# A 4-layer transformer block stack on one core: natural query and key rows, heads split at the eviction, a reworked block inversion and new order tables

## The chip, the cores and the metric

The kernel is one program on one core of a Trainium2 chip. The metric is the device time of one execution in microseconds (us). Everything is float32, apart from two small masks in bfloat16.

## The reference, cut to what matters

64 sequences of 128 tokens and 128 channels pass through four layers; each layer is an attention, a cross-attention on a context of 77 tokens and a feed-forward part, each with a residual and a layer norm:

```python
x = _layernorm(x + _L0_attn_ref(x, ...))        # "rec": a recurrence over the tokens, called memory below
x = _layernorm(x + _L0_xattn_ref(ctx, x, ...))  # "x0": 16 heads of 8 channels, softmax
x = _layernorm(x + _L0_ffn_ref(x, ...))         # "f0": routed experts
x = _layernorm(x + _L1_attn_ref(x, ...))        # "a1": latent attention
x = _layernorm(x + _L1_xattn_ref(x, ctx, mask)) # "x1": 16 heads of 8, masked
x = _layernorm(x + _L1_ffn_ref(x, ...))         # "f1"
x = _layernorm(x + _L2_attn_ref(x, ...))        # "a2": 16 heads of 8
x = _layernorm(x + _L2_xattn_ref(x, ctx, ...))  # "x2": 16 heads of 8, masked
x = _layernorm(x + _L2_ffn_ref(x, ...))         # "f2"
x = _layernorm(x + _L3_attn_ref(x, ...))        # "a3": 16 heads of 8, rotary
x = _layernorm(x + _L3_xattn_ref(x, ctx, ...))  # "x3": relu attention
x = _layernorm(x + _L3_ffn_ref(x, ...))         # "f3": conv, 16 heads of 8, gated experts
```

The heads of 8 channels are what the first part of the change touches: six stages (x0, x1, a2, x2, a3, f3) compute `softmax(q k^T) v` for 16 heads of 8 channels. The recurrence of `rec` needs, for each sequence, the inverse of a unit triangular system of 128 tokens, which the kernel solves in four blocks of 32 tokens; this is the second part.

## The kernel before, in words

There are two phases. The **opening** (`opening`, class `Memory`, from the start to 463.6 us) works on all 64 sequences at once and computes the memory `z` of `rec`, which goes to DRAM; beside it run steps that prepare weights (`Setup`, `setup_*`). The **main part** (`decoder_phase`) handles 16 batches of 4 sequences. Three groups (threads 0, 1, 2) hold one batch each and walk through the twelve stages; their instructions are interleaved on every engine by a table written out by hand into the file (`ORDER`, one character for each step of a thread; `MEMORY_ORDER` for the opening; `in_order` runs them). The order on an engine is fixed, so an instruction that waits holds up all three threads. `BATCH` lists the steps of a batch on each engine and gives the semaphore values, `GIVEN` says which pair of PSUM banks goes to which stage.

**The opening.** From 0 to 84 us the keys of all sequences are made (`keys_*_of`, three threads). Then come four blocks of 32 tokens:
- `g` is copied from PSUM (L1078), stored to DRAM and loaded back as `E`, one sequence in each of 64 partitions (L1128, L1132).
- The elimination (`memory_vector`, L1083 to L1099) takes 31 steps j. With n = 31 - j each is a chain of four VectorE instructions: a reciprocal (L1087), a column of n values (L1090), an outer product n x n into `outer` (L1093) and a subtraction n x n (L1097). GpSimd (`memory_gpsimd`, L1045 and L1049) carries the inverse along: an outer product and a subtraction of n x (j + 1) values in each step, which wait for the column of L1090.
- VectorE turns the inverse into `xx` twice, negated and scaled (L1104, L1107). It is stored (L1135) and loaded back by eight DMAs into the diagonal blocks of a 128 x 128 operand `xs` (L1143).
- TensorE multiplies with it (`next_pairs`, L955; 128 rows, 32 matmuls for four chunks of 4 x 4 sequences each), ScalarE and VectorE copy each chunk (L1014, L1071), `next_diagonal` (L970) completes the next `g`.
- Beside the elimination of the next block runs what is left of this one (`rest_tensor`, `rest_scalar`: L863 to L884, L899 to L910) and `early_diagonal` (L922, L926).

After the fourth block 16 products (L997) give the last part of `z`; it stays in `uT`, which is stored whole, 4 MB (L1152), and the main part begins.

**The attention stages.** Each of 16 heads has 8 rows, and a matmul of the scores works on a 32-row strip of queries and keys (L1525, L1551). For that the queries and keys are projected with padded weights: two matmuls, one for each half of the heads (t = 0, 1), with zero rows between (`queries_tensor` L1495, `keys_tensor` L1426); in a3 four each, since the rotary partner is a projection too (L2387). ScalarE evicts each half of the queries with its bias (L1504). Of the keys VectorE evicts the first half (L1443) and ScalarE the second (L1440), two copies each, one for every head of a pair, with the other head's rows zeroed. The maxima of the scores (L1617) go to free rows of `tops`, are transposed by one TensorE instruction (L1537) and added to both halves of the queries (L1620), after which the scores are computed a second time, keys first, with the maximum subtracted (L1551), and exponentiated (L1604).

```python
for t in range(2):                                     # queries_tensor, L1492 to L1496
    e.matmul(b.bank[st][t][:, :], g.w.part(st + "_q", t), src, ...)
```

## Time and profile before

| | us |
|---|---|
| median of 3 runs | 5462.85 (5457.16 to 5479.28) |
| profiled execution | 5466.28, its span 5464.1 |
| opening, to the first DMA issue of the main part | 463.6 |
| main part | 5000.5 |
| granted TensorE clock, mean | 0.94 |

| engine | busy us | share |
|---|---|---|
| TensorE matmul | 4782.4 | 88% |
| VectorE | 3585.9 | 66% |
| ScalarE | 2303.5 | 42% |
| GpSimd | 705.7 | 13% |

How to read it: a float32 matmul leaves two records in the trace, a transpose leaves one. Records of TensorE overlap, so its busy time is less than count times mean. In views by line, each group gives busy time and mean duration of one record, and after the bar the idle time before it and what ended that. "L1495" is line 1495 of the kernel. The span starts at the first instruction.

### The profile page before, as it was taken

What the parts mean: (1) busy time and instruction counts of PE and PEld (TensorE: products, weight loads), DVE (VectorE), ACT (ScalarE), POOL (GpSimd) and SP (SyncE); (2) the same over time, 40 slices, a digit from 0 to 9 for tenths busy, and PEclk for the clock granted to TensorE, in tenths of its full rate; (3) what the DMA queues carried; (4) which work ended last, traced back from release to release, by engine and by line L of the source; (5) the groups of instructions that cost most, each with busy time, mean ns of one, the idle gap of its engine ahead of it and who ended that gap; (6) DMA issues with size and microseconds to landing.
All of it is one profiled execution on the core that took longest, in us unless ns stands there. A gap on an engine that the chain in (4) does not pass through costs nothing.

```text
span 5464.1 us, 130532 instructions
## 1 busy us (share of the span) xinstructions
PE 4782.4 (88%) x55217; PEld 3486.1 (64%) x55217; DVE 3585.9 (66%) x9609; ACT 2303.5 (42%) x4635; POOL 705.7 (13%) x738
## 2 busy tenths in 40 slices
PE   5574889899998989999999999999999989988787
PEld 4453666566766666776766676666676766666555
DVE  7664477666667676667776576767767677756643
ACT  3111344444434454453554444454445355343432
POOL 5452000101000010110010010011110010100010
PEclk7676899999999999999999999999999999999998
DMA  1103101011110101111100111010021110110001
GB/s 61 23 17 105 58 7 32 2 32 31 51 53 20 32 3 40 60 44 41 33 2 19 41 54 48 26 33 15 28 63 41 32 33 10 32 43 22 2 24 37
DMA packets 144930, 184.57 MB, mean 34 GB/s; under 512 B 46074, under 2 KB 73826, under 8 KB 143714
## 3 DMA queue, kind: packets, MB, share of 16 engines
q1 hardware_dynamic: 144354, 176.23, 10.7%
q8 instruction: 442, 7.24, 0.5%
q14 instruction: 134, 1.10, 0.1%
HBM read 164.32 MB, written 11.57 MB: 32 GB/s over the span
## 4 chain that ended last, share of the span: by engine, by line
PE 63%; DVE 12%; issue 7%; ACT 6%; POOL 1%; DMA 1%; SPq 1%; POOLq 0%; DVEq 0%; ACTq 0%
PE g_bank L2649 8%; PE g_bank L2664 8%; PE g_bank L1551 6%; PE g_bank L1574 5%; PE g_bank L1525 4%; ACT g_keys_exps L1604 4%; DVE g_tops L1617 3%; PE g_bank L1495 2%; PE g_bank L1901 2%; PE g_bank L1911 2%; PE g_bank L2387 2%; PE g_bank L1426 2%; PE g_bank L1381 1%; PE g_bank L1994 1%; PE g_bank L2249 1%
## 5 line engine op out<-in xcount | busy, mean ns | idle before, releaser
L1604 ACT ACTIVATE g_keys_exps<-g_bank 128x512 f32<-128x512 f32 (+1 forms) x1536 | 796.0, 596 | 601.6 <-PE g_bank L1551 600.8
L1617 DVE TENSOR_REDUCE g_tops<-g_bank 128x4 f32<-128x512 f32 (+1 forms) x1536 | 808.5, 575 | 318.9 <-PE g_bank L1525 316.6
L1360 POOL TENSOR_TENSOR g_rstd<-g_rstd,minus_half 128x4 f32<-128x4 f32 x224 | 227.2, 1015 | 4144.2 <-DVE g_rstd L1342 4103.0
L2664 PEld LDWEIGHTS g_bank<-region,g_keys_exps 128*128 128x128 f32 x4096 | 517.3, 192 | 151.4 <-issue 140.6
L2649 PE MATMUL g_bank<-g_xT,region 128*128 128x512 f32 x1024 | 550.7, 619 | 8.6 <-DVE g_keys_exps L2689 4.2
L2664 PE MATMUL g_bank<-region,g_keys_exps 128*128 128x128 f32 x4096 | 546.4, 278 | 3.7 <-DVE g_base L2696 3.7
L1551 PE MATMUL g_bank<-g_qa,g_keys_exps 32*77 32x128 f32 (+1 forms) x12288 | 455.8, 285 | 53.7 <-DVE g_o L1638 34.2
L1551 PEld LDWEIGHTS g_bank<-g_qa,g_keys_exps 32*77 32x77 f32 (+1 forms) x12288 | 379.8, 169 | 158.8 <-DVE g_o L1638 57.0
L1574 PE MATMUL g_bank<-g_keys_exps,g_v 77*32 77x128 f32 (+1 forms) x12288 | 430.7, 283 | 39.7 <-DVE g_tops L1617 28.9
L1525 PE MATMUL g_bank<-g_keys_exps,g_qa 32*128 32x154 f32 (+1 forms) x6144 | 389.3, 365 | 77.3 <-ACT g_keys_exps L1604 67.4
L1574 PEld LDWEIGHTS g_bank<-g_keys_exps,g_v 77*32 77x32 f32 (+1 forms) x12288 | 324.8, 112 | 145.3 <-DVE g_tops L1617 84.7
L1525 PEld LDWEIGHTS g_bank<-g_keys_exps,g_qa 32*128 32x128 f32 x6144 | 262.1, 189 | 190.5 <-ACT g_keys_exps L1604 112.1
L2677 ACT ACTIVATE g_keys_exps<-g_bank,region 128x512 f32<-128x512 f32 x256 | 176.0, 687 | 447.5 <-PE g_bank L2649 447.2
L2689 DVE TENSOR_SCALAR g_keys_exps<-g_bank,region 128x512 f32<-128x512 f32 x256 | 191.5, 748 | 241.5 <-PE g_bank L2649 240.3
L1598 ACT ACTIVATE g_oT_sc<-g_bank 128x256 f32<-128x256 f32 x384 | 146.8, 383 | 373.0 <-PE g_bank L1574 372.6
L1620 DVE TENSOR_TENSOR g_qa<-g_qa,g_bank 128x256 f32<-128x256 f32 x384 | 159.9, 416 | 180.2 <-PE g_bank L1537 177.7
L1369 ACT ACTIVATE g_x<-g_x,g_shift,g_rstd 128x128 f32<-128x128 f32 x384 | 170.5, 488 | 160.5 <-DVE g_shift L1346 159.4
L2649 PEld LDWEIGHTS g_bank<-g_xT,region 128*128 128x128 f32 x1024 | 158.5, 192 | 59.2 <-issue 45.7
L1635 DVE RECIPROCAL g_total<-g_bank 128x16 f32<-128x16 f32 x384 | 95.9, 250 | 131.7 <-PE g_bank L1585 131.0
L1585 PE MATMUL g_bank<-consts_sb,g_oT_sc 128*128 128x128 f32 x768 | 159.5, 292 | 23.1 <-ACT g_keys_exps L1604 11.7
L1335 DVE BATCH_NORM_STATS2 g_stats<-g_x 128x6 f32<-128x128 f32 x768 | 176.5, 279 | 3.6
L2696 DVE SCALAR_TENSOR_TENSOR g_base<-g_bank,g_gates,g_base 128x128 f32<-128x128 f32 x512 | 149.3, 342 | 43.3 <-PE g_bank L2664 38.4
(375 smaller groups left out, 8771.3 us busy)
## 6 DMA issues: line engine op xcount, KB each, us to landing
region<-L_w_in SPq DMA_DIRECT2D x512, 256.0 KB, 3.0
region<-xT_in SPq DMA_DIRECT2D x16, 256.0 KB, 2.7
z_scratch<-m_uT SPq DMA_DIRECT2D x1, 4096.0 KB, 11.0
g_oT_sc<-z_scratch SPq DMA_DIRECT2D x16, 256.0 KB, 3.0
g_xT<-xT_in SPq DMA_DIRECT2D x16, 256.0 KB, 3.9
g_o<-x_in SPq DMA_DIRECT2D x16, 256.0 KB, 4.0
out<-g_x SPq DMA_DIRECT2D x16, 256.0 KB, 2.4
region<-weights_in SPq DMA_DIRECT2D x1, 3020.5 KB, 10.2
```

The lines of the kernel that those rows point to most:

```text
L1335: e.bn_stats(g.stats[:, n, :], src[:, n, :]).then_inc(*b.vector(f"{st} stats {n}"))
L1360: e.tensor_tensor(g.rstd[:, :], g.rstd[:, :], g.s["minus_half"], ALU.pow).then_inc(*b.gpsimd(st + " rstd"))
L1369: e.activation(out[:, n, :], src[:, n, :], ACT.Identity, bias=g.shift[:, n:n + 1], scale=g.rstd[:, n:n + 1]).then_inc(*b.scalar(f"{st} nor ...
L1525: ins = e.matmul(bank[r][:, 2 * nk * t:2 * nk * (t + 1)].rearrange("p (i k) -> p i k", i=2), g.qa[rows, t, n, :], g.km[rows, n, t, :, 0:nk ...
L1551: ins = e.matmul(bank[r][0:nk, u * T:(u + 1) * T], g.km[rows, n, t, i, 0:nk], g.qa[rows, t, n, :], start=not masked, stop=not masked or u ...
L1574: ins = e.matmul(b.bank[st][0][32 * u:32 * u + 32, k * T:(k + 1) * T], g.v[0:nk, n, 8 * i + 4 * k + u, :], g.p[0:nk, 2 * i + k, u, :], sta ...
L1604: e.activation(g.p[0:nk, r, :, :], bank[r][0:nk, :].rearrange("p (u q) -> p u q", u=4), ACT.Exp, scale=scale).then_inc(*b.scalar(f"{st} p ...
L1617: e.tensor_reduce(g.tops[:, first:first + 4].rearrange("p (t i) -> p t i", t=2), src, AX, ALU.max).then_inc(*b.vector(f"{st} top {n} {r}"))
L2649: e.matmul(bank[0][:, :], weights.part(f"w1 {x}", c), g.xT, start=True, stop=True).then_inc(*b.tensor(f"f3 hidden {k}"))
L2664: ins = e.matmul(bank[1][:, n * D:(n + 1) * D], g.gated_hid[:, x % 2, c, n * T:(n + 1) * T], weights.part(f"w2 {x}", c), start=c == n == 0 ...
L2677: e.activation(g.gated_hid[:, k // HC % 2, k % HC, :], b.bank["ex"][0][:, :], ACT.Relu, bias=g.w["f3_b1"][:, k:k + 1]).then_inc(*b.scalar( ...
L2689: e.tensor_scalar(g.gated_hid[:, x % 2, k % HC, :], b.bank["ex"][0][:, :], g.w["f3_b1"][:, k:k + 1], 0.0, ALU.add, ALU.max).then_inc(*b.ve ...
```

## The change

Three things are changed together.

1. *Natural rows.* Head h keeps its own 8 rows of the 128 (32-row strips hold four heads, t is their half of the strip). Queries and keys are projected once with the plain weights; the split is made where PSUM is evicted, with a per-partition scale that is 1 or 0 (`half` for queries, `own_head` for keys). x1 keeps two key projections, because its mask needs two rows (`own_or_mask`). In x0 and x2 all four key copies are ScalarE's; in a2 and f3 ScalarE's two wait for VectorE's two, since both read one bank; a3 has four projections rather than eight, four products with the rotary table rather than eight, two additions on GpSimd rather than four, and ScalarE makes the two halves of the queries from SBUF. The maxima lie in different free rows for the two halves, so they are transposed by two instructions rather than one.
2. *The opening.* The column of a step is no VectorE instruction: ScalarE makes it for GpSimd (`columns_scalar`), and VectorE's outer product takes the reciprocal as its scalar (`scalar_tensor_tensor`); for n up to 22 it is written to PSUM. The inverse is kept transposed in two buffers `XT`, with the reciprocals in a 33rd column, and is stored as it is, 264 KB; two DMAs (1,024 pieces of 132 bytes each) bring it back to a compact `xs`. Products use 32-row, 32-column tiles. The scaling by the reciprocals is done where V and s are made. z is transposed by TensorE, kept for one block (`z`) and stored block by block, so that 1 MB is left at the end; a batch loads it by four DMAs. The solve of the next four sequences is issued ahead of the rows of the current ones (`solve_tensor`). The stores and loads of a block come ahead of the ten small setup DMAs on SyncE's queue. ScalarE's table places one column step after every one to three steps of its other work.
3. *Tables.* `MEMORY_ORDER`, `ORDER`, `GIVEN`, `BATCH` and `SETUP` are new. `ORDER` has 5,056 TensorE steps rather than 5,264, 4,176 rather than 4,080 of ScalarE, 8,640 rather than 8,768 of VectorE, 400 rather than 432 of GpSimd.

The diff, cut to its core (the tables are left out):

```diff
-def queries_tensor(e, b, st, src, first, second):
-    g = b.g
+def queries_tensor(e, b, st, src, ready):
+    e.wait_ge(*ready)
+    e.matmul(b.bank[st][0][:, :], b.g.w[st + "_q"], src, start=True, stop=True).then_inc(*b.tensor(st + " q"))
+    yield
+def queries_scalar(e, b, st):
+    g = b.g
+    e.wait_ge(*b.tensor[st + " q"])
     for t in range(2):
-        for mark in (first, second)[t]:
-            e.wait_ge(*mark)
-        e.matmul(b.bank[st][t][:, :], g.w.part(st + "_q", t), src, start=True, stop=True).then_inc(*b.tensor(f"{st} q {t}"))
-        yield
+        e.activation(g.qa[:, t, :, :], seqs(b.bank[st][0][:, :]), ACT.Identity, bias=g.w[st + "_bq"][:, t:t + 1],
+                     scale=g.k["half"][:, t:t + 1]).then_inc(*b.scalar(f"{st} q {t}"))
+        yield
+def context_keys_scalar(e, b, st):
+    e.wait_ge(*b.tensor[st + " k"])
+    for t in range(2):
+        yield from keys_of_tile(e, b, st, t, S2, keys_read(b, st, 0, S2), b.g.w[st + "_bk"], b.scalar, True)
+def own_keys_scalar(e, b, st):
+    e.wait_ge(*b.vector[st + " k 0 1"])
+    yield from keys_of_tile(e, b, st, 1, T, keys_read(b, st, 1, T), b.g.w[st + "_bk"], b.scalar, True)
...
-        e.transpose(bank[2][:, 0:T], g.tops[:, :], g.k["ident"]).then_inc(*b.tensor(f"{st} tops turned {n}"))
+        for t in range(2):
+            ins = e.transpose(bank[2][:, t * T:(t + 1) * T], top_rows(g, t), g.k["ident"])
+        ins.then_inc(*b.tensor(f"{st} tops turned {n}"))
...
-    for name, out in (("q", g.turned), ("k", k_turned)):
-        for i in range(4):
+    for name, out in (("q", g.turned[0:2]), ("k", g.turned[2:4])):
+        for i in range(2):
             e.wait_ge(*b.tensor[f"a3 {name} {i}"])
...
-            e.reciprocal(me.rd[:, 0:1], me.E[:, j, j:j + 1]).then_inc(me.chain, 1)
+            e.reciprocal(XT[:, j, BLK:BLK + 1], me.A[:, j, j:j + 1]).then_inc(me.chain, 1)
             yield
             e.wait_ge(me.chain, steps + 1)
-            e.tensor_scalar(me.cols[:, j, 0:n], me.E[:, j + 1:, j], me.rd[:, 0:1], None, ALU.mult).then_inc(me.chain, 1)
+            e.scalar_tensor_tensor(out=outer, in0=over(me.A[:, j + 1:, j], 2, n), scalar=XT[:, j, BLK:BLK + 1],
+                                   in1=over(me.A[:, j, win], 1, n), op0=ALU.mult, op1=ALU.mult).then_inc(me.chain, 1)
             yield
...
+def columns_scalar(e, me):
+    for blk in range(NBLK):
+        for j in range(BLK - 1):
+            n = BLK - 1 - j
+            e.wait_ge(me.chain, chain_steps(blk, j) + 1)
+            e.activation(me.cols[:, j, 0:n], me.A[:, j + 1:, j], ACT.Copy, scale=me.XT[blk % 2][:, j, BLK:BLK + 1]
+                         ).then_inc(me.cols_set, 1)
+            yield
...
     for q in range(4 * c, 4 * c + 4):
-        e.wait_ge(me.rows_set, blk * me.nq + q + 1)
-        out = slice(q % 4 * BLK, (q % 4 + 1) * BLK)
-        for k in range(2):
-            ins = e.matmul(me.bank[PAIR_BANKS[c][k]][:, out], me.xs[:, q, k, :], me.rows[:, q, at:at + BLK],
+        for j in range(4):
+            lane = slice(32 * j, 32 * j + 32)
+            ins = e.matmul(pairs_in(me, c)[lane, q % 4, :], me.xs[lane, q, 0:BLK], me.rows[lane, q, at:at + BLK],
                            start=True, stop=True)
...
-        for j in range(4):
-            for k in range(2):
-                ...
-                e.dma_start(me.xs[32 * j:32 * j + 32, :, k, 32 * j:32 * j + 32],
-                            dram["xx"].rearrange("(q j) k (a m) -> j a k q m", j=4, a=2)[j, k]
-                            ).then_inc(me.xs_loaded, 16)
+        for half in range(2):
+            ...
+            e.dma_start(me.xs[:, 8 * half:8 * half + 8, :],
+                        dram["xx"].rearrange("(q j) k m -> (j k) q m", j=4)[:, 8 * half:8 * half + 8, :]
+                        ).then_inc(me.xs_loaded[half], 16)
...
-    e.dma_start(g.oT, seqs(dram["z"][:, first * T:(first + SEQS) * T])).then_inc(g.arrived["z"], 16)
+    for blk in range(NBLK):
+        e.dma_start(g.oT[:, :, cols_of(blk)], dram["z"][:, blk, at, :]).then_inc(g.arrived["z"], 16)
```

## Rows read from the trace of the kernel before

**Rows 1.** Page, part 1: busy us (share of the span) x instructions

```profile
PE 4782.4 (88%) x55217; PEld 3486.1 (64%) x55217; DVE 3585.9 (66%) x9609; ACT 2303.5 (42%) x4635; POOL 705.7 (13%) x738
```

**Rows 2.** Stretches: length, busy us by engine, then clock, DMA share, GB/s

```profile
700.00:4800.00 4100.00, 3792.51 (x44320) 2774.76 (x44319) 2840.37 (x7655) 1900.61 (x3645) 396.34 (x364) 0.98 0.11 32
4800.00:5464.00 664.00, 553.42 (x5387) 379.76 (x5387) 347.21 (x962) 229.73 (x436) 52.36 (x48) 0.93 0.08 25
0.00:464.00 464.00, 256.62 (x3697) 196.75 (x3697) 296.61 (x697) 93.17 (x402) 229.16 (x289) 0.70 0.18 50
...
5000.00:5200.00 200.00, 156.75 (x1966) 105.70 (x1963) 122.33 (x334) 82.19 (x160) 19.76 (x18) 0.88 0.02 5
```

**Rows 3.** The same view over block 1 of the opening and its end

```profile
190.00:250.00 60.00, 39.84 (x686) 26.72 (x678) 55.55 (x133) 14.21 (x60) 46.13 (x62) 0.78 0.01 2
250.00:260.00 10.00, 0.42 (x1) 0.18 (x1) 3.15 (x12) 1.06 (x3) 0.00 (x0) 0.50 0.58 105
260.00:277.00 17.00, 16.98 (x194) 16.60 (x195) 4.05 (x10) 1.11 (x4) 0.00 (x0) 0.50 0.00 1
...
452.00:464.00 12.00, 0.00 (x0) 0.00 (x0) 0.00 (x0) 0.00 (x0) 0.40 (x1) 0.54 0.81 350
```

**Rows 4.** Timeline of SyncE's queue, opening: start us, us of issuing, DMAs

```profile
151.41 8.56 SPq L3137 DMA_DIRECT2D f_val<-setup_val  x10
...
250.05 0.52 SPq L1135 DMA_DIRECT2D xx_scratch<-m_xx  x1
254.29 4.03 SPq L1143 DMA_DIRECT2D m_xs<-xx_scratch  x8
277.23 0.38 SPq L1128 DMA_DIRECT2D g_scratch<-m_g  x1
...
451.76 0.34 SPq L1152 DMA_DIRECT2D z_scratch<-m_uT  x1
```

**Rows 5.** Groups by line on VectorE, 190 to 250 us: busy, mean ns

```profile
L1097 DVE TENSOR_TENSOR m_E<-m_E,m_outer 64x961 f32<-64x961 f32 (+30 forms) x31 | 21.6, 696 | 1.1
L1093 DVE TENSOR_TENSOR m_outer<-m_cols,m_E 64x961 f32<-64x961 f32 (+30 forms) x31 | 15.5, 501 | 1.1
L1090 DVE TENSOR_SCALAR m_cols<-m_E,m_rd 64x31 f32<-64x31 f32 (+30 forms) x31 | 9.3, 301 | 1.1
L1087 DVE RECIPROCAL m_rd<-m_E 64x1 f32<-64x1 f32 x31 | 4.8, 155 | 1.1
```

**Rows 6.** Timeline of GpSimd in block 1: first, 23rd and last step

```profile
190.62 1.11 POOL L1045 TENSOR_TENSOR m_inv_outer<-m_cols,m_E 64x31 f32<-64x31 f32 x1 [43.14 <-DVE m_cols L1090]
...
236.25 0.53 POOL L1045 TENSOR_TENSOR m_inv_outer<-m_cols,m_E 64x207 f32<-64x207 f32 x1 [0.17 <-DVE m_cols L1090]
...
245.28 0.23 POOL L1045 TENSOR_TENSOR m_inv_outer<-m_cols,m_E 64x31 f32<-64x31 f32 x1 [0.22 <-DVE m_cols L1090]
```

**Rows 7.** Timeline of TensorE behind block 1's inverse

```profile
260.02 7.04 PE L955 MATMUL m_bank<-m_rows,m_xs 128*128 128x32 f32 x32 [7.58 <-DMA m_xs<-xx_scratch]
266.99 0.65 PE L970 MATMUL m_bank<-region,m_V 32*32 32x32 f32 x32
```

**Rows 8.** Groups by line and shape on TensorE, 700 to 4900 us; then two timeline rows

```profile
L1495 PE MATMUL g_bank<-g_xT,region 128*128 128x512 f32 x286 | 143.8, 608 | 2.7 <-ACT g_xT L1403 2.1 <-DVE g_v L1742 0.4 <-ACT g_xT L2574 0.2
L1537 PE MATMUL g_bank<-consts_sb,g_tops 128*128 128x128 f32 x343 | 102.2, 298 | 38.8 <-DVE g_tops L1617 37.1
L1426 PE MATMUL g_bank<-g_ctxT,region 128*128 128x308 f32 x168 | 58.2, 444 | 0.0
...
924.96 1.98 PE L2387 MATMUL g_bank<-g_xT,region 128*128 128x512 f32 x4
...
1218.83 0.60 PE L1381 MATMUL g_bank<-consts_sb,g_x 128*128 128x128 f32 x4
```

**Rows 9.** The same groups on ScalarE and VectorE

```profile
L1440 ACT ACTIVATE g_keys_exps<-g_bank,region,consts_sb 128x308 f32<-128x308 f32 x84 | 47.5, 611 | 36.8 <-PE g_bank L1426 20.3 <-PE g_bank L1429 16.3
...
L2410 DVE TENSOR_TENSOR g_keys_exps<-g_bank,consts_sb 128x512 f32<-128x512 f32 x84 | 57.0, 684 | 22.9 <-PE g_bank L2387 22.4
```

**Rows 10.** What TensorE waited for, 700 to 4800 us: total, times, longest

```profile
PE g_bank L1525 <- ACT g_keys_exps L1604: 51.9, 62, 2.7
PE g_bank L1678 <- DMA g_xT<-xT_in: 30.9, 10, 4.4
```

889 lines of the change are left out of this document (470 added, 419 removed), and 190 rows, old and new, of tables (BATCH, SETUP).

## The prediction

> **What bounds the kernel now.** I read five views, from coarse to fine. The page's first part shows TensorE busy for 88% of the span, VectorE for 66%, ScalarE for 42% [rows 1]. The view by stretches shows that this is two regimes. In the main part TensorE is busy for 3792.5 of 4100 us, 92.5%, at a clock of 0.98, while VectorE stands at 69% and ScalarE at 46%; in the opening TensorE is busy for 257 of 464 us, at 0.70 [rows 2]. What TensorE waits for in the main part is scattered: the largest item is 51.9 us in 62 waits, of 307 us of idleness [rows 10]. So the main part is bound by the length of TensorE's queue, and what is taken off that queue should show almost whole. The finer view of the opening shows a chain: in block 1 VectorE is busy for 55.6 of 60 us and TensorE idles or has slack; then the DMAs run for 10 us with all engines nearly idle; then TensorE works for 17 us at a clock of 0.50 while nothing else can; at the end 12 us are one transfer at 350 GB/s [rows 3]. The opening is a chain of latencies, not of throughput. I cost the two parts apart.
>
> **The profiled execution.** It took 5466.3 us: a span of 5464.1 (463.6 of opening, 5000.5 of main part) and 2.2 around it. It lies 3.4 us above the median of the runs shown, so I make the sum against 5466.3 and take 3 off at the end.
>
> **Main part, what leaves TensorE.** A batch loses eleven projections of 512 columns: one of queries in x0, x1 and x2 each, one of queries and one of keys in a2 and in f3 each, four in a3. It loses two of 308 columns (keys of x0 and x2). A projection is two records. By busy time one costs 143.8/286 x 2 = 1.01 us, one of 308 columns 58.2/168 x 2 = 0.69 us; two in a row hold the engine for 1.98 us with the tail of the last, which puts the distance between two at about 0.86 to 0.95 [rows 8]. I take 0.86 as what the queue gets back, and 0.6 for the narrow ones: 11 x 0.86 + 2 x 0.6 = 10.7 us a batch. By busy time it would be 12.5.
>
> **What TensorE gains.** The maxima are transposed by two instructions: 6 stages x 4 sequences = 24 more a batch. One alone is 0.30 us, but four in a row take 0.60, so each further one costs (0.60 - 0.27)/3 = 0.11 [rows 8]; they sit in front of L1620, which waits for both. 24 x 0.11 = 2.6 us. Net 8.1 us a batch, 129 us in 16 batches; by busy time 12.5 - 2.6 = 9.9, or 158 us, and 158/0.925 = 171 if the idleness shrank in proportion. That is the upper bound.
>
> **The other engines in the main part.** VectorE loses four key copies in x0 and x2 (nearest row: ScalarE's own copy of the same shape, 0.61) and four products in a3 at 0.68 each, about 5 us a batch. ScalarE gains those four copies at 0.61 and two query halves in a3 (nearest row the 0.61 of the narrower copy, upper bound 0.9 for 512 columns from SBUF), together 4 us a batch, 64 us in all on an engine that idles for 54% of the stretch [rows 2, 9]. The scale that is now an operand of the query eviction is also one of L1440, whose 308 columns take 0.61; I price it at nothing, at most 0.1 x 10 a batch. GpSimd loses two additions in a3. The cover of ScalarE's additions is the work of the two other threads; without it 64 us would come back, but not all on TensorE's path, as they stand before stages whose partner threads have matmuls ready.
>
> **New waits.** ScalarE's keys in a2 and f3 now wait for VectorE's two copies, some 1.4 us; behind them in ScalarE's queue stand the exponentials of the other threads, which TensorE already waits for (51.9 us in 62 waits, [rows 10]). The price is between 0 and 2 x 1.4 x 16 = 45 us; I take 10. The three further loads of z in a batch cost SyncE 3 x 0.45 us of issue; they come long before the load of xT that TensorE waits for (30.9 us in 10 waits, [rows 10]); at the start of the main part they are bare, 1.4 to 2.7 us. Their pieces are 128 bytes; at 8% to 11% DMA share [rows 2] nothing queues behind them. I take 120 of the 129 us, with 60 (half lost to waits) and 171 as ends.
>
> **Opening, the elimination.** In a block VectorE's four kinds take 21.6 + 15.5 + 9.3 + 4.8 = 51.2 us and 124 gaps of 0.035, 55.5 in all [rows 5]. Without the column it is 55.5 - 9.3 - 1.1 = 45 us, if the product with a scalar costs what the plain one does (no row shows its n x n form, from below I see no gain, from above 0.06 for a write to PSUM in 22 steps, 1.3 us). But GpSimd has two instructions in each step. They were hidden: 1.11 us for 31 values beside VectorE's large product, 0.23 when it is alone, 0.53 for 207 values [rows 6], which makes about 0.19 + 0.0016 for each value. In the late steps that engine becomes the later one. The first 15 steps are VectorE's: 34.3 us now, 29.6 without the columns. The last 16 are GpSimd's at 0.8 to 1.5, mean 1.15 (2 x 0.53 + gaps of 0.25 in the 23rd): 18.4. Sum 48 us, and the store of the inverse follows at once, where it now follows at 60.0, after L1104 and L1107. That is 11.5 a block, 46 in four; between 32 (ScalarE's column, held up behind its evictions of the rest, makes every late step 0.2 slower) and 60.
>
> **Opening, between the blocks.** Block 1 now takes 27.2 us from the store of the inverse to the store of g (250.05 to 277.23, [rows 4]): 4.2 to land, 5.7 for eight loads, 16.5 for products and copies, 0.8 for the copy of g. After: 3.1 for the smaller store, 0.5 + 2.5 for two loads, then tiles of 32 x 32, of which 32 records take 0.65 at the low clock against 7.04 for 32 of the large ones [rows 7]; with two evictions in each chunk, pipelined, 3.5; the copy 0.8: 10.4. I add 1.3, as `early_diagonal` now ends close to it, since ScalarE's table spreads the rest over the whole elimination. Gain 15.5, twice. Block 0 has the ten setup DMAs in front of its loads, 8.56 us [rows 4]; it takes 32.4 and gains 21.5. The last block takes 28.5 from its store to the main part (435.05 to 463.6), of which 12 are the 4 MB transfer [rows 3, 4]: 3.1 + 3.0 + 5 for 64 narrow products + 1.8 for evictions + about 4.6 for 1 MB (between 3.0 for 256 KB and 11 for 4 MB) = 17.5, gain 11. Together 63.5. With the elimination 109.5; I take off 10, because ScalarE's queue now ties TensorE's rest to the steps, and 2 for the loads of z: 98, with 75 and 120 as ends.
>
> **Shared interface.** The rows show VectorE and GpSimd hinder one another: 1.11 us for 31 values beside VectorE's product, 0.23 later [rows 6], and L1097 takes 6 us a block more than L1093 of the same sizes [rows 5]. The Trainium skill, "GPSIMD Engine Reference", Key points, says that GpSimd shares its SBUF interfaces with VectorE and that the contention is with instructions in a two-port mode or with two SBUF inputs. The trace agrees as far as these two rows go. By that rule the subtraction, whose second input for n up to 22 now lies in PSUM, would run free of it; the page's rule is the mechanism of the third rival.
>
> **Rivals.**
> - *The elimination does not get shorter* (12%). The columns stand in ScalarE's queue behind evictions that wait for TensorE at a half clock, and GpSimd waits for them. For it: four or five steps of ScalarE's other work go with every two columns. Against: TensorE is busy for 40 of 60 us in block 1 [rows 3] and loses work. The 46 us are lost: 5466.3 - 52 - 120 - 3 = 5291.
> - *The waits take what the queue gives back* (12%). The main part is then bound by the latency of three threads, not by TensorE. For it: the second score waits for a chain of six steps, none shorter. Against: 92.5% busy. A gain of 25: 5466.3 - 98 - 25 - 3 = 5340.
> - *VectorE and GpSimd come apart for n up to 22* (5%): subtractions cost like products, 6 us a block less on VectorE and 3 on GpSimd's side, which is the later one: 12 us in all, 5233.
> - *Slower, by the clock* (3%). Where TensorE is busy for 78%, its mean clock is 0.88, against 0.98 at 92.5% [rows 2]: part of that time was granted at 1.2 rather than 2.4 GHz. If the thinner queue made the whole stretch from 700 to 4800 like that, its 3792 us would take 0.98/0.88 as long, 431 more, against 218 gained: 5676. It decides from the point where 218/3792 = 5.7% is lost, a mean clock below 0.93 in that stretch. The Trainium skill, "TensorE: Matmul & The Clock Gate", HAM oscillation, describes such a fall after idle gaps. Against it: the idle time per wait stays below 3 us for most.
>
> That nothing happens at all is excluded by the number of instructions that leave; I keep 1% for within 0.5%.
>
> **The numbers.** Forecast 5466.3 - 98 - 120 - 3 = 5245 us, 67%, its own range 5180 to 5310. The range of 8 in 10 goes from 5175 (both upper bounds nearly: 5466.3 - 120 - 168 - 3) to 5335, nearly all of the second rival's centre. Faster by over 0.5% (what a measurement of this kernel can tell from none): 0.95. Within: 0.01. Slower: 0.04.
>
> **What would show it.** L1426, L1495 and L2387 have 26 records a batch fewer (416 in all), the transposes 384 more. TensorE's busy time falls by 125 to 160 us in the main part at 92% and a clock of 0.98. The opening ends near 366 us; between the first reciprocal and the store of the inverse lie 48 to 50 us, with GpSimd's last instruction the later one; from that store to the store of g 11 to 12. The prediction is wrong if TensorE's share of the main part falls below 90%, if the order tables hold new waits of more than 3 us each, or if the columns wait for ScalarE.

## The result, and the profile after

The changed kernel takes 5400.2 us (median of 4 runs, 5384.2 to 5404.5), the kernel before 5461.0 beside it: a ratio of 0.9877, 95% interval 0.9846 to 0.9907. The medians lie 61 us apart, where 218 were forecast and 5335 was the upper end of the range. The ratio compares means rather than medians and makes it 67 us (51 to 84). Below, a ratio is turned into us with 5461. The kernel before was run again beside each set of experiments, not always on the same chip (its medians lie between 5459 and 5478 us), so kernels of different sets are compared by their ratios and not by their medians. One execution of a later experiment (xT ahead of the store too) took 6114.7 us at a granted clock of 0.72 and is left out of its numbers, as a slow one.

Most of what is missing stands in the main part. This is the view by stretches of the changed kernel (length, busy us of PE, PEld, DVE, ACT, POOL, then TensorE's clock, DMA share, GB/s): opening, main part, and the stretch that [rows 2] shows of before.

```profile
0.00:375.20 375.20, 232.12 (x4169) 147.35 (x4169) 250.83 (x561) 123.26 (x526) 208.62 (x296) 0.69 0.19 55
375.20:5402.40 5027.20, 4446.68 (x51488) 3258.21 (x51488) 3210.49 (x8784) 2264.98 (x4329) 432.64 (x418) 0.96 0.11 32
700.00:4800.00 4100.00, 3700.77 (x43689) 2725.65 (x43689) 2717.95 (x7447) 1925.81 (x3690) 357.54 (x336) 0.97 0.11 32
```

And the main part of the kernel before, in the same view:

```profile
463.60:5464.10 5000.50, 4525.78 (x51520) 3289.32 (x51520) 3289.26 (x8912) 2210.30 (x4233) 476.95 (x450) 0.96 0.11 32
```

The opening ends at 375.2 rather than 463.6 us: 88 of the 98 us forecast. The main part, forecast 120 us shorter, is 27 us longer. TensorE is busy for 79 us less in it (4525.8 to 4446.7), and idle for 106 us more (474.7 to 580.5). So the work did leave the queue, and the time didn't follow. TensorE's share of the main part fell from 90.5% to 88.5%, and in the stretch of [rows 2] from 92.5% to 90.3%; the granted clock of that stretch was 0.97, from 0.98.

Part 1 of the page of the changed kernel answers to [rows 1]: TensorE and VectorE have less to do, ScalarE more.

```profile
PE 4678.8 (87%) x55657; PEld 3405.6 (63%) x55657; DVE 3461.3 (64%) x9345; ACT 2388.2 (44%) x4855; POOL 641.3 (12%) x713
```

What TensorE waited for in the changed kernel, 700 to 4800 us (total, times, longest), answers to [rows 10]. The first row had been 51.9 us in 62 waits, the last 30.9 in 10.

```profile
PE g_bank L1617 <- ACT g_keys_exps L1698: 66.3, 81, 2.7
PE g_bank L1630 <- DVE g_tops L1720: 38.5, 52, 2.6
PE g_bank L1781 <- DMA g_xT<-xT_in: 36.4, 11, 4.6
```

TensorE's groups, 700 to 4900 us, answer to [rows 8] (records | busy us, mean ns of one | idle before). L1630, the transposition of the maxima, has twice the records and 139.0 rather than 102.2 us; so each further one takes 0.11 us, as forecast; the projections L1587 and L2489 have half.

```profile
L1630 PE MATMUL g_bank<-consts_sb,g_tops 128*128 128x128 f32 x673 | 139.0, 289 | 39.5 <-DVE g_tops L1720 38.5
L1587 PE MATMUL g_bank<-g_xT,region 128*128 128x512 f32 x138 | 75.8, 632 | 6.5 <-ACT g_xT L1473 6.5
L2489 PE MATMUL g_bank<-g_xT,region 128*128 128x512 f32 x112 | 59.2, 637 | 3.5 <-ACT g_xT L1473 2.4 <-DVE g_keys_exps L2509 1.1
```

The opening went nearly as forecast. SyncE's queue around the inverse of block 1 (answers to [rows 4]):

```profile
211.54 0.50 SPq L1205 DMA_DIRECT2D xx_scratch<-m_XT  x1
214.51 1.88 SPq L1212 DMA_DIRECT2D m_xs<-xx_scratch  x2
216.44 0.57 SPq L1179 DMA_DIRECT2D z_scratch<-m_z  x1
224.09 0.36 SPq L1196 DMA_DIRECT2D g_scratch<-m_g  x1
```

VectorE's elimination of that block, 160 to 212 us, by line (answers to [rows 5]):

```profile
L1153 DVE SCALAR_TENSOR_TENSOR m_bank<-m_A,m_XT 64x484 f32<-64x484 f32 (+21 forms) x22 | 13.2, 599 | 0.8
L1157 DVE TENSOR_TENSOR m_A<-m_A,m_outer 64x961 f32<-64x961 f32 (+8 forms) x9 | 9.3, 1033 | 0.3
L1153 DVE SCALAR_TENSOR_TENSOR m_outer<-m_A,m_XT 64x961 f32<-64x961 f32 (+8 forms) x9 | 8.8, 977 | 0.3
L1157 DVE TENSOR_TENSOR m_A<-m_A,m_bank 64x484 f32<-64x484 f32 (+21 forms) x22 | 7.2, 325 | 0.8
L1150 DVE RECIPROCAL m_XT<-m_A 64x1 f32<-64x1 f32 x31 | 4.8, 155 | 1.1
```

The first reciprocal starts at 161.56 and the store of the inverse at 211.54: 50.0 us, forecast 48 to 50. GpSimd's last subtraction ends at 211.52 and releases the store, as forecast. From that store to the store of g lie 12.55 us, forecast 11 to 12.

### The profile page after: what moved, and what is told of

Its sections match the earlier page's. It is cut to its first block, busy times and chain, and to the rows that moved or that the text cites. A ratio compares the mean times of both kernels' runs of the same rounds, so it can differ in the third digit from the quotient of the medians.

```text
span 5402.4 us, 131265 instructions
## 1 busy us (share of the span) xinstructions
PE 4678.8 (87%) x55657; PEld 3405.6 (63%) x55657; DVE 3461.3 (64%) x9345; ACT 2388.2 (44%) x4855; POOL 641.3 (12%) x713
## 4 chain that ended last, share of the span: by engine, by line
PE 62%; DVE 15%; ACT 8%; issue 5%; DMA 1%; POOL 1%; SPq 1%; POOLq 0%; DVEq 0%; ACTq 0%
PE g_bank L2750 8%; PE g_bank L2765 8%; PE g_bank L1645 6%; PE g_bank L1617 5%; ACT g_keys_exps L1698 5%; PE g_bank L1668 5%; DVE g_tops L1720 4%; PE g_bank L2013 2%; PE g_bank L2003 2%; PE g_bank L1630 2%; PE g_bank L1451 1%; PE g_bank L1679 1%; PE g_bank L2096 1%; PE g_bank L2351 1%; PE g_bank L2332 1%
## 5 line engine op out<-in xcount | busy, mean ns | idle before, releaser
L1630 PE MATMUL g_bank<-consts_sb,g_tops 128*128 128x128 f32 x768 | 159.6, 291 | 51.3 <-DVE g_tops L1720 49.8
L1679 PE MATMUL g_bank<-consts_sb,g_oT_sc 128*128 128x128 f32 x768 | 161.2, 295 | 27.3 <-ACT g_oT_sc L1692 12.5
```

The lines of the kernel that those rows point to most:

```text
L1630: ins = e.transpose(bank[2][:, t * T:(t + 1) * T], top_rows(g, t), g.k["ident"])
L1679: ins = e.transpose(b.bank[st][1][:, k * P:(k + 1) * P], outputs_of(g, n)[:, k, :], g.k["ident"])
```

## The experiments

The theories, in the order in which they came. A: the new order table is bad. B: the latency of the three threads is the bound, whatever the queue. C, formed after the first runs: a fixed order is one longest path (the chain of instructions and waits that sets the end), and a table is balanced for its own durations, so that work taken away shows less than work added. D: TensorE's queue isn't on that path in the kernel before. E and F: the load of z does or doesn't hold up the load of xT.

**The old order with the new steps.**

```diff
-ORDER, GIVEN = the changed kernel's
+ORDER, GIVEN = those of the kernel before, its removed steps taken out, its new steps put before the next of their thread
```

> The changed kernel, with ORDER and GIVEN of the kernel before carried over: each step that is left keeps its place among the steps of the three threads, an added step stands just before the next step of its own thread. Everything else is as changed. Theory A (the new order table interleaves the threads less well, the lighter steps themselves are worth what was forecast): the main part takes 4880 to 4930 us rather than 5027, the whole some 5270 to 5300, with TensorE's stalls in the main part back near 774. Theory B (the main part is bound by the latency of three threads, whatever the order): the main part stays at 5000 to 5060, the whole at 5375 to 5430.

Measured: 5379.7 us, ratio 0.9839 (0.9811 to 0.9867). The new table isn't what took 120 us; it is 21 us slower than the old one, carried over without any planning. The two intervals overlap, but two later pairs of runs that differ in the table alone show the same sign, 47 and 26 us, clear of the noise. The main part takes 5010 us, in theory B's interval.

**The queue made shorter, alone.**

```diff
-        e.matmul(b.bank[st][t][:, :], ..., src, ...)
+        out, of = (b.bank[st][1][:, 0:16], src[:, 0, 0:16]) if t and st[0] == "x" else (b.bank[st][t][:, :], src)
+        e.matmul(out, ..., of, ...)             # and a3's projections 2 and 3 likewise
```

> The kernel before with seven projections a batch cut from 512 columns to 16, the second half of the queries of x0, x1 and x2 and four of the eight of a3; the evictions read the first half's bank instead, so those heads get wrong values. Nothing else changes: same steps, same order. It takes 7 x 0.86 = 6.0 us of TensorE's queue a batch, 96 us in all. If the queue is the bound, the time falls by 80 to 105 us to 5355 to 5380. If the latency of the threads is (theory B), it falls by less than 35 us. Theory A says as the first.

Measured: 5460.8 us, ratio 0.9986 (0.9967 to 1.0005): 8 us for 96. Its main part:

```profile
465.20:5458.90 4993.70, 4484.40 (x51520) 3297.23 (x51520) 3285.01 (x8912) 2209.19 (x4233) 477.25 (x450) 0.96 0.11 32
```

TensorE's busy time fell by 41 us (4525.8 to 4484.4) and its idle time rose by 35 (474.7 to 509.3). Busy time fell by less than the 96 us of queue for two reasons that can be read and not told apart in size: the groups that were not touched take longer per record (the scores of L1525, 416 ns rather than 409), and a busy interval ends with the tail of its last matmul, so more waits make busy time too. The idle time rose in part at the cut matmuls themselves: the projections of a3 wait for VectorE to free their bank for 6.8 us in 12 waits, from 0.9 in 2. The mean granted clock over the runs is 0.933, in the runs of before beside them 0.9385; 0.0056 of 5461 us is 31 us of TensorE's full speed. So up to a third of the 88 us that don't show may be clock; whether the clock fell by itself or because the engine waited more is open. The forecast's first sentence on the main part, that what is taken off the queue should show almost whole, is false in this kernel.

**The queue made longer, alone.**

```diff
+            e.matmul(b.bank[st][t][:, :], g.w.part(st + "_q", t), src, start=True, stop=True)   # once more: x0, x1, x2, and four of a3
```

> The kernel before with seven projections a batch issued twice (the second half of the queries of x0, x1, x2 and four of a3): the mirror of before_cut, 96 us more of TensorE's queue in the same order. Theory C (formed after before_cut and after_doubled: a fixed order is one longest path; the order table is balanced for its own durations, so that TensorE's queue and the chain of waits between the engines end together; work taken away shows nearly nothing, work added nearly whole): 70 to 96 us more than before. Theory D (TensorE's queue isn't on the path at all in the kernel before, and only the new table is sensitive to it): less than 30 us more.

Measured: 5553.3 us, ratio 1.0152 (1.0132 to 1.0173): 83 us for 96. Its main part:

```profile
467.80:5544.90 5077.10, 4609.73 (x51744) 3330.55 (x51744) 3288.02 (x8912) 2211.63 (x4233) 477.29 (x450) 0.97 0.10 32
```

Busy 84 us more, idle 7 us less. The same seven matmuls in the same places: added they cost 83 us, taken away they bring 8. It lies in theory C's interval, and D falls; B, in the form that the queue doesn't matter, falls too.

**The queue made longer in the changed kernel.**

```diff
+    e.matmul(b.bank[st][0][:, :], b.g.w[st + "_q"], src, start=True, stop=True)   # all 13 projections a batch twice
```

> The changed kernel, with each of the 13 projections a batch that the change had taken away issued again (the remaining projection is issued twice into the same bank), in the order table of the changed kernel. It adds 11 x 0.86 + 2 x 0.6 = 10.7 us of queue a batch, 171 us in all. If the queue is the bound: 5400 + 150 to 175. Theory B (latency): less than 60 us more. Theory A with stalls that come of a bad table lets part of it vanish in the stalls: 60 to 140 more.

Measured: 5547.9 us, ratio 1.0147 (1.0124 to 1.0170): 147 us more than the changed kernel for 171, just under the interval of the queue as the bound. With the new table, too, work added shows nearly whole.

**The same in the old order.** The edit is the last one, on top of the first.

> The changed kernel with ORDER and GIVEN of the kernel before, and the 13 projections a batch that were taken away issued again. TensorE then has the queue of the kernel before plus the second transpositions (42 us), in the order of the kernel before; what differs is where key copies and query halves are made (ScalarE rather than VectorE) and their waits. If these moves cost nothing: main part 5040 us, the whole 5410 to 5425. If they are what took the gain (new waits on the latency chain): 5450 to 5500. In the new order table the same work took 5548.

Measured: 5501.0 us, ratio 1.0060 (1.0037 to 1.0082). It has the projections of the kernel before in the order of the kernel before, and an opening that is 90 us shorter, and yet it is 33 us slower than before. So some 120 us come from what else changed. The 13 projections are worth 1.0060 - 0.9839, or 121 us, of 171.

**The chain made shorter, alone.**

```diff
-            src = bank[r][:, 0:4 * nk].rearrange("p (t i k) -> p t i k", t=2, i=2)
+            src = bank[r][:, 0:4 * nk].rearrange("p (t i k) -> p t i k", t=2, i=2)[:, 0:1, :, :]
```

> The kernel before with VectorE's maxima taken over half of the columns (256 rather than 512, or 154 rather than 308), so that the four reductions of each round end about 1 us earlier; the second half of the heads gets no maximum and the exponentials are scaled down. TensorE's queue is untouched. If the latency of a thread alone were the bound: 24 rounds a batch, 1 us each, three threads: 8 us a batch, 128 us less. Theory C: 10 to 50 us less, since the queue is as late. If the queue alone is the bound: within 10 us.

Measured: 5409.6 us, ratio 0.9887 (0.9865 to 0.9908), 62 us less with TensorE's work untouched. Its main part:

```profile
464.20:5406.80 4942.60, 4497.07 (x51520) 3280.76 (x51520) 2974.94 (x8912) 2209.57 (x4233) 476.75 (x450) 0.97 0.11 33
```

VectorE, an engine that stood at 66% [rows 1], is busy for 314 us less, and this buys 62 us where 96 us taken off TensorE's queue bought 8. It lies above theory C's interval of 10 to 50 us and far below the 128 of the chain as the only bound: the chain counted for more than C had expected. What TensorE waits for between 700 and 4800 us shows where it was gained: the wait for the maxima ahead of their transposition fell from 36.5 us in 52 waits to this, while that of L1525 for the exponentials grew from 51.9 to 64.3.

```profile
PE g_bank L1537 <- DVE g_tops L1617: 11.7, 12, 1.9
```

**Both.** The two edits together.

> The kernel before with both edits, the seven projections cut and the maxima over half of the columns. Theory C: now both paths are shorter, 80 to 140 us less than before, clearly more than the two alone together. If the latency of the threads is the bound alone: as before_short (its gain within 20 us). If the granted clock takes back what the queue gives (the mean clock falls as TensorE is busy for less): a gain under 60 us and a mean clock under 0.93.

Measured: 5387.4 us, ratio 0.9853 (0.9832 to 0.9874): 80 us, at the lower edge of theory C's interval. The cut is worth 18 us once the chain is shorter, rather than 8; the intervals overlap, so that a shorter chain makes the queue count for more is suggested and not shown; the two edits together are not clearly more than their sum of 70 us, as theory C had expected. The mean granted clock over the runs fell from 0.941 to 0.9365.

**The second transposition, in the changed kernel and in the kernel before.**

```diff
-        for t in range(2):
-            ins = e.transpose(bank[2][:, t * T:(t + 1) * T], top_rows(g, t), g.k["ident"])
+        ins = e.transpose(bank[2][:, 0:T], top_rows(g, 0), g.k["ident"])
```

> The changed kernel with one transposition of the maxima rather than two; the second half of the queries gets no maximum of its own and the exponentials are scaled down so that nothing overflows. It leaves 24 transposes a batch out, 0.11 us each by the forecast: 42 us of queue in all, and 0.11 us of the chain scores, maxima, transposition, shift, scores in each of 24 rounds. Queue as bound: 35 to 45 us less than the changed kernel. Theory B: up to 24 x 0.14 x 6 rounds of three batches = 20 us less. If a second transposition costs more than forecast (its own weight load of 128 rows): 60 us or more less.

Measured: 5394.4 us, ratio 0.9864 (0.9840 to 0.9887); against the changed kernel 7 us less, give or take 21. Once more work taken away shows nothing that can be measured, and the 35 to 45 us of the queue as the bound are excluded. The other direction:

```diff
+        e.transpose(bank[2][:, T:2 * T], g.tops[:, :], g.k["ident"])
         e.transpose(bank[2][:, 0:T], g.tops[:, :], g.k["ident"]).then_inc(*b.tensor(f"{st} tops turned {n}"))
```

> The kernel before with one thing of the change: the maxima are transposed by two instructions (the second result isn't used). 24 more a batch, 42 us of TensorE's queue by the forecast's 0.11 us each. Theory C (work added to a balanced order shows nearly whole): 35 to 45 us more than before. If each costs more than forecast, because it stands in the chain of every round and not only in the queue: 55 to 80 us more. If it is hidden in the stalls: less than 15.

Measured: 5482.7 us, ratio 1.0042 (1.0027 to 1.0056): 23 us, less than forecast and below theory C's interval of 35 to 45. Not all work added shows nearly whole.

**The wait of ScalarE's own keys.**

```diff
+    if st in ("a2", "f3"):
+        e.wait_ge(*b.vector[st + " k 0 1"])
```

> The kernel before with one thing of the change: in a2 and f3 ScalarE's two key copies wait for VectorE's two. The forecast priced it at 10 us, between 0 and 45. If the new waits are what took the gain of the main part: 30 to 60 us more. If the wait is covered: within 10 us.

Measured: 5464.8 us, ratio 1.0006 (0.9992 to 1.0020). Nothing.

**The context keys on ScalarE.**

```diff
+def first_keys_scalar(e, b, st):                       # ahead of keys_scalar in x0 and x2; keys_vector goes
+    e.wait_ge(*b.tensor[st + " k 0"])
+    yield from keys_of_tile(e, b, st, 0, S2, src, b.g.w[st + "_bk"], b.scalar, True)
```

> The kernel before with one thing of the change: in x0 and x2 ScalarE makes all four key copies, VectorE none; they stand just before ScalarE's other two of the same thread, and the order tables are adapted in these steps alone. The forecast priced it at nothing. If ScalarE's 4 x 0.61 us a batch are covered: within 10 us of before. If they stand in the chain (TensorE's transposition behind a2 and rec now waits for all four, and exponentials of the other threads queue behind them): 20 to 40 us more.

Measured: 5479.0 us, ratio 1.0029 (1.0015 to 1.0044): 16 us, between the two cases. As profiled the main part is 12.8 us longer, and TensorE is idle for only 1.7 us more in it; its busy time grew by 11.1 with as many records as before. The mean granted clock over the runs was 0.938, beside 0.940 of before.

**The rotary stage.**

```diff
-    for t in range(2):                     # GpSimd makes both halves of the queries
-        e.tensor_tensor(g.qa[:, t, :, :], g.turned[2 * t], g.turned[2 * t + 1], ALU.add)
+    e.tensor_tensor(g.turned[0], g.turned[0], g.turned[1], ALU.add)
+    ...                                    # ScalarE, ahead of its two key copies:
+    for t in range(2):
+        e.activation(g.qa[:, t, :, :], g.turned[0], ACT.Copy, scale=...)
```

> The kernel before with the rotary stage a3 of the change: four products with the rotary table rather than eight, one addition on GpSimd for the queries rather than two and one for the keys, and ScalarE makes both halves of the queries from SBUF, two steps behind the addition. The four projections are issued twice, so that TensorE's queue is as before (the layout stays padded, so the second half of the heads gets the first half's values). If ScalarE's two steps, which stand between the addition and the scores, are what is missing: 20 to 50 us more than before. If VectorE's four products fewer pay for them, as the forecast took: within 10 us, or less than before.

Measured: 5508.8 us, ratio 1.0079 (1.0063 to 1.0096): 43 us, with 64 products on VectorE fewer. The edit also issues the projections in pairs on one bank and changes what they wait for, so it is the stage that is measured, and not the two copies by themselves. ScalarE's timeline in the first batch's a3, kernel before (start, us, line, what, count [idle before]):

```profile
937.13 0.66 ACT L2437 ACTIVATE g_v<-g_bank 128x256 f32<-128x256 f32 x2 [0.68 <-PE g_bank L2392]
937.67 1.51 ACT L1440 ACTIVATE g_keys_exps<-g_keys_exps,consts_sb 128x512 f32<-128x512 f32 x2
939.75 2.06 ACT L1604 ACTIVATE g_keys_exps<-g_bank 128x512 f32<-128x512 f32 x4 [0.56 <-PE g_bank L1551]
```

and with the rotary stage of the change:

```profile
944.47 0.66 ACT L2435 ACTIVATE g_v<-g_bank 128x256 f32<-128x256 f32 x2 [0.67 <-PE g_bank L2395]
945.01 1.33 ACT L2439 ACTIVATE g_qa<-g_keys_exps,consts_sb 128x512 f32<-128x512 f32 x2
946.24 1.51 ACT L1442 ACTIVATE g_keys_exps<-g_keys_exps,consts_sb 128x512 f32<-128x512 f32 x2
947.65 2.04 ACT L1606 ACTIVATE g_keys_exps<-g_bank 128x512 f32<-128x512 f32 x4
```

The two halves take 1.33 us ahead of the keys, and the four exponentials of another thread, for which ScalarE had waited 0.56 us behind the keys, now stand ready behind them without a gap. That the 43 us come from such delays is not shown, and TensorE's waits speak against it. Its main part, as profiled:

```profile
463.90:5512.40 5048.50, 4557.44 (x51520) 3313.89 (x51520) 3240.53 (x8848) 2230.67 (x4265) 434.81 (x418) 0.96 0.10 32
```

It is 48 us longer than that of before; 32 of these are TensorE's busy time, with as many records, and 16 its idle time. TensorE's wait for the exponentials, L1527 here, is what it was: 67.5 us in 80 waits in the whole main part, from 67.4 in 82. What grew is the wait for the key copies that stand behind the two halves, from 1.0 us in 2 waits to 5.2 in 7. The mean clock was 0.9335, beside 0.939 of before; by the reckoning above that is 29 us. So most of the cost stands in TensorE's busy time and not in its waits, and its cause is open.

**The opening alone.** The changed opening, the main part of the kernel before.

```diff
-    e.dma_start(g.oT, seqs(dram["z"][:, first * T:(first + SEQS) * T])).then_inc(g.arrived["z"], 16)
+    for blk in range(NBLK):
+        e.dma_start(g.oT[:, :, cols_of(blk)], dram["z"][:, blk, at, :]).then_inc(g.arrived["z"], 16)
```

This is the only edit that reaches into its main part.

> The changed opening with the main part of the kernel before (its weights, its steps, its order tables; z is loaded in four pieces, as the changed opening stores it). If opening and main part are independent, as the forecast assumed: 5463 - 90 = 5370 to 5380 us, which would be as fast as the changed kernel in the order of before (5380) and faster than the changed kernel (5400). If the four loads of z or the earlier start of the main part cost something: up to 5395.

Measured: 5402.2 us, ratio 0.9891 (0.9872 to 0.9910), outside the expected interval. The opening gains 91 us (it ends at 372.7), the whole 60. Its main part is 29 us longer than that of before:

```profile
372.70:5402.10 5029.40, 4533.39 (x51520) 3298.48 (x51520) 3287.66 (x8912) 2212.59 (x4233) 476.41 (x450) 0.96 0.11 32
```

TensorE's wait for xT, 700 to 4800 us, went from 30.9 us in 10 waits [rows 10] to this:

```profile
PE g_bank L1807 <- DMA g_xT<-xT_in: 47.5, 12, 5.4
```

Why shows in SyncE's queue at a change of batch. Kernel before:

```profile
1252.37 0.45 SPq L2889 DMA_DIRECT2D g_ctxT<-ctxT_in  x1
1252.86 0.43 SPq L2893 DMA_DIRECT2D g_oT_sc<-z_scratch  x1
1253.34 1.97 SPq L2897 DMA_DIRECT2D g_xT<-xT_in  x1
```

Changed kernel, the same place:

```profile
1175.26 0.43 SPq L2991 DMA_DIRECT2D g_ctxT<-ctxT_in  x1
1175.74 2.09 SPq L2996 DMA_DIRECT2D g_oT_sc<-z_scratch  x4
1177.87 0.51 SPq L3000 DMA_DIRECT2D g_xT<-xT_in  x1
```

All loads of a batch are issued in one burst behind the store of the last one. The four pieces of z take 2.09 us rather than 0.43 and stand straight ahead of xT, for which TensorE waits.

**xT ahead of the other loads.**

```diff
     g, at = b.g, slice(first, first + SEQS)
+    if b.turn:
+        e.wait_ge(*b.tensor.before(f"f3 hidden {EXPERTS * HC - 1}"))
+    e.dma_start(g.xT, seqs(dram["xT"][:, first * T:(first + SEQS) * T])).then_inc(g.arrived["xT"], 16)
+    yield
     ...                                    # the five other loads, without this one
```

In the changed kernel:

> The changed kernel with one edit: SyncE issues the load of xT first of a batch's six, ahead of mask, dots, context and the four pieces of z, rather than behind them. It is then issued 3.3 us earlier in each of the 13 batches that follow another one. Theory E (the four pieces of z delay xT, for which TensorE waits 46 us in 12 waits, and each such wait is on the longest path): 20 to 45 us less than the changed kernel, 5355 to 5380, TensorE's wait for xT under 15 us. Theory F (the main part is longer for another reason, a lower clock or the balance of the path): the wait for xT shrinks and others grow in its place, 5390 to 5405.

Measured: 5362.3 us, ratio 0.9791 (0.9768 to 0.9813), 47 us less than the changed kernel. In the old order:

> The same edit in the changed kernel with the order of the kernel before (which took 5380). Theory E: 5335 to 5360. Theory F: 5370 to 5385.

Measured: 5340.1 us, ratio 0.9744 (0.9723 to 0.9764), 52 us less than without it. TensorE's wait, 700 to 4800 us:

```profile
PE g_bank L1781 <- DMA g_xT<-xT_in: 3.5, 4, 2.4
```

In the kernel before:

> The kernel before with xT loaded first of a batch's six (it is now behind mask, dots, context and one piece of z, 1.65 us). By the 3.3 us and 47 to 52 us that the same edit brought in the changed kernel: about half of it, 20 to 30 us less than before. If the kernel before had the queue covered: within 10 us.

Measured: 5434.1 us, ratio 0.9939 (0.9923 to 0.9956): 33 us. So two thirds of this cost was in the kernel before, and the change added the other 14 to 19 us. Three pieces more at 0.55 us, in 13 changes of batch, make 21.

**xT ahead of the store too.**

```diff
+        if after:
+            load_xT(e, after, dram, after.index * SEQS)
         yield from store_sync(e, b, dram, b.index * SEQS)
```

> The changed kernel with the order of the kernel before, and the load of xT of the next batch issued ahead of the store of the current one: SyncE then waits for the last projection of the experts (f3 hidden 31), not for the end of the batch. Theory E: TensorE's wait for xT goes to nearly nothing, 5325 to 5355, below xt_first_old_order. Theory F: 5370 to 5385.

Measured: 5325.1 us (three executions), ratio 0.9730 (0.9696 to 0.9764): not told apart from xt_first_old_order, so that it comes out below that one isn't shown. With the main part of before:

> The changed opening with the main part of the kernel before (5402), and the load of xT issued ahead of the store. Theory E: the 30 us that the main part had gained come back, and the wait for xT of the kernel before (31 us in 10 waits) goes too: 5335 to 5370. Theory F: 5395 to 5405.

Measured: 5356.6 us, ratio 0.9772 (0.9747 to 0.9797), 65 us less than the same kernel without it (0.9891). TensorE's wait for xT between 700 and 4800 us is 0.2 us there, from 47.5. Theory F falls in all five runs; theory E has the sign right each time, with gains at the upper end of what was expected or above it (47 us for 20 to 45, 33 for 20 to 30). With xT ahead in both, the changed opening is worth 0.9939 - 0.9772, or 91 us, all that it is shorter by. So the late xT accounts for the whole 31 us that the opening alone had been missing, if early and first are worth the same, as they were, within the noise, in the changed kernel. The two kernels with the changed steps, the order of before and xT early (0.9744 and 0.9730) are the fastest here, faster than both kernels of the case.

## Why the prediction was wrong, point by point

*The profiled execution, and the opening.* Right in the main, 88 of 98 us; it ends at 375 rather than 366. The elimination: 50.0 us in block 1, GpSimd the later one, its last steps without a wait, so the columns did not hold it up. Over four blocks, from the store of g to that of the inverse, 36 us were gained rather than 46, and between the blocks 54 rather than 63.5. Between the blocks: 12.55 us in block 1. Block 2 took 17.0 from store to store rather than 12 to 12.5; in TensorE's timeline two stretches of 2.2 and 1.6 us there wait for nothing that the profile shows:

```profile
293.92 0.48 PE L1006 MATMUL m_bank<-region,m_V 32*32 32x32 f32 x18 [2.17 <-issue]
...
297.61 0.97 PE L1006 MATMUL m_bank<-region,m_V 32*32 32x32 f32 x54 [1.55 <-issue]
```

The end took 18.8, forecast 17.5. VectorE's part had another shape, and came out even: the product by a scalar costs more than the plain one (22.0 us in all rather than the 15.5 of [rows 5]), the subtraction less (16.5 rather than 21.6).

*What leaves and joins TensorE's queue.* Counted right: 416 records fewer and 384 more, 51520 to 51488 in the main part.

*What that is worth.* This step failed. It said that at 92.5% busy the queue is the bound and that what leaves it shows almost whole. 96 us taken away brought 8, the same 96 added cost 83. The 13 projections, 171 us of queue, brought 121 in the old order, on top of steps that had made the kernel 33 us slower; so what a removal brings depends on what stands beside it. The reasoning from the busy share was wrong in kind: TensorE was idle 475 us of the main part in many small waits, and each busy stretch that gets shorter ends sooner in such a wait (35 us more of them in the run with 96 taken away). At this balance 92.5% busy says that additions hurt. It doesn't say that removals help. The forecast had the rival, "the waits take what the queue gives back", and gave it 12% with a gain of 25 us; its price came from nothing, and more was lost beside it.

*The forecast's own signs.* It called itself wrong if TensorE's share of the main part fell below 90%. It fell to 88.5%, though before it had been 90.5% and not the 92.5% of the stretch. Busy time fell by 79 us rather than 125 to 160. The largest groups of waits for other engines stay below 3 us each, at 2.7 and 2.6, as the forecast wanted. But there are more of them: TensorE's waits in the main part rose by 54 us for ScalarE and by 42 for VectorE.

*The second transpositions.* Forecast 42 us, measured 23.

*The other engines.* This step failed too. ScalarE's additions were priced at nothing because it idles for 54% of the stretch. Context keys: 16 us. Rotary stage: 43 us. Both put copies, as the rows of the rotary stage show for one of them, into ScalarE's queue ahead of exponentials. But in neither run did TensorE's wait for the exponentials grow; most of the time came as TensorE's busy time at a slightly lower clock, so that the price is shown and its path is not. The own wait measured 3 us rather than 10.

*The loads of z.* The forecast said that they come long before the load of xT. They stand directly ahead of it: the timeline that it had read for the opening [rows 4] shows the same queue in the main part, and wasn't read there. Forecast 2 us, measured 14 to 19 for the pieces with the changed steps. With the main part of before they cost 31, of which 29 show in the profiled main part of that run, and all of it goes when xT is issued ahead.

*The order tables.* Priced at nothing. Against the old order the new one is 21 us slower, within the noise by itself; with the projections doubled 47 (1.0147 against 1.0060), with xT first 26 (0.9791 against 0.9744).

The sum by the runs, each part measured alone in the kernel before, the projections and the table on the changed steps:

| part of the change | forecast | measured |
|---|---|---|
| opening, with its loads of z | -98 | -60 |
| 13 projections a batch fewer | -171 | -121 |
| second transpositions | +42 | +23 |
| own wait | +10 | +3 |
| context keys on ScalarE | 0 | +16 |
| rotary stage | 0 | +43 |
| new order table | 0 | +21 |
| sum | -217 | -75 |
| the change | | -67 (0.9877) |

The measured parts are known to 8 to 23 us each. Of the 142 us between the two sums, 59 are ScalarE's additions, 50 the projections, 38 the opening with its loads and 21 the order table; 26 came back from the transpositions and the own wait, which had been priced too high. The rows of the projections and of the table are steps between kernels that have all the rest, so they add up by construction. The one test of the sum is the rest: rows one and three to six, each measured by itself, give +25 for the changed kernel in the old order with doubled projections; it measured +33.

*The clock rival.* Its mechanism was seen at a small size. With TensorE's work cut the mean clock fell by 0.0056, with the rotary stage by 0.0054; with seven projections added it stayed (0.9377 beside 0.9373). No run that a ratio rests on came near the 0.88 that the rival had used: the changed kernel had 0.97 in the stretch from 700 to 4800 us, and the rival needed less than 0.93. Its mean over the runs, 0.945, didn't fall either, with 88 us less of an opening at 0.7. The Trainium skill, "TensorE: Matmul & The Clock Gate", HAM oscillation, describes a lower clock after idle gaps; these runs agree in sign, and which gaps did it is not shown.

*VectorE and GpSimd.* The rival's mechanism was there too: the subtraction of 484 values, which reads PSUM now, took 650 ns, from 906 before (rows at the end). It brought nothing: over the 22 steps the subtractions fell from 12.4 to 7.2 us and the products, whose inputs both lie in SBUF, rose from 7.3 to 13.2. And GpSimd was the later one.

## What to carry to other kernels

In a kernel with a fixed order on each engine, measure the slope before forecasting from the busy share: issue the instruction in question twice, and once shortened. Here the same matmuls were worth 83 us one way and 8 the other, and shorter reductions on an engine that was busy for 66% brought 62.

Read each in-order queue where it meets the next batch. Three more DMAs of 0.55 us each stood ahead of the one load that TensorE waits for; moving that load to the head of the burst gave 33 us in the kernel before and 47 to 52 in the changed one, where the whole change brought 67.

A copy moved to a half-idle engine isn't free: on ScalarE, at 46%, two such moves cost 16 and 43 us where nothing had been forecast. Look for the cost in the busy time and the clock of the engine that bounds the kernel too, and not only in its waits.

## What of the hardware had not been expected

The product by a scalar of its partition whose result goes to PSUM took 0.74 us for 64 values and 0.66 for 25, while those of 81 and 36 values took 0.30 and 0.25. The rows in VectorE's timeline of the changed kernel, block 1:

```profile
200.86 0.30 DVE L1153 SCALAR_TENSOR_TENSOR m_bank<-m_A,m_XT 64x81 f32<-64x81 f32 x1
...
201.65 0.74 DVE L1153 SCALAR_TENSOR_TENSOR m_bank<-m_A,m_XT 64x64 f32<-64x64 f32 x1
...
203.59 0.25 DVE L1153 SCALAR_TENSOR_TENSOR m_bank<-m_A,m_XT 64x36 f32<-64x36 f32 x1
204.28 0.66 DVE L1153 SCALAR_TENSOR_TENSOR m_bank<-m_A,m_XT 64x25 f32<-64x25 f32 x1
```

GpSimd's timeline in the same place:

```profile
201.69 0.62 POOL L1117 TENSOR_TENSOR m_XT<-m_XT,m_inv_outer 64x220 f32<-64x220 f32 x1
...
204.32 0.57 POOL L1117 TENSOR_TENSOR m_XT<-m_XT,m_inv_outer 64x192 f32<-64x192 f32 x1
```

Each of the two slow products starts 0.04 us before an instruction of GpSimd and ends 0.05 to 0.08 us after it. From 361 down to 121 values the product takes 0.76 to 0.86 us whatever its size, where the plain one of the kernel before took 0.53 to 0.28, and each ends 0.15 to 0.40 us after the GpSimd instruction that ran or began at its start, the sooner the smaller it is. That is what a product that waits for GpSimd's instruction would look like; no run tests it.

The subtraction is faster by 28% with one operand in PSUM, while GpSimd works beside it. VectorE's groups by shape, kernel before:

```profile
L1097 DVE TENSOR_TENSOR m_E<-m_E,m_outer 64x484 f32<-64x484 f32 x1 | 0.9, 906 | 0.0
```

and the changed kernel:

```profile
L1157 DVE TENSOR_TENSOR m_A<-m_A,m_bank 64x484 f32<-64x484 f32 x1 | 0.7, 650 | 0.0
```
